# A four-layer conv, scan and attention network, 64 samples on one core: new order of VectorE's four instructions per state pair, ScalarE's table loads and the work around them

## What is computed

```python
# layer 0: 1x1 expand 96 -> 576 + silu, 5x5 depthwise conv with weights mixed per
#          sample + silu, gate (squeeze-excite), 1x1 conv back to 96, residual
# layer 1: group norm, projection to 192, 3x3 depthwise conv + silu -> xc, then
def step(h, inps):                       # 768 channels, n = 16 states each
    u_t, dt, B_t, C_t = inps
    dA = jnp.exp(dt[:, :, None] * A)                         # "decay"
    h = dA * h + (dt * u_t)[:, :, None] * B_t[:, None, :]    # "drive", the scan
    y = jnp.einsum('bdn,bn->bd', h, C_t) + Dv * u_t          # "product", summed over n
    return (h, y)
_, ys = jax.lax.scan(step, h0, xs)       # over the 784 pixels
#          y1 + y2 + y3 + y4, layer norm, times silu(z), projection, residual
# layer 2: layer norm, FFT mixer over the pixels, FFN in fp8/fp16 rounding
# layer 3: layer norm, attention without softmax, FFN
```

## Time and profile before

| | |
|---|---|
| time, median of 3 runs | 22538.34 us (22494.2 to 22542.6) |
| the profiled execution: time; its span | 22505.68 us; 22503.9 us |
| busy share: VectorE, TensorE, ScalarE, GpSimd | 86%, 84%, 69%, 28% |
| granted TensorE clock, mean | 0.894 |
| VectorE per pair | 2 scans of 1.79 and 1.78 us, drive 0.96 us, product 0.96 us |

### The profile page before, as it was taken

How to read it: one execution, slowest core, us unless ns; L and a number is a source line. 1 busy time by engine, 2 the same in 40 slices (tenths; PEclk the granted TensorE clock), 3 DMA queues, 4 the chain that set the end, 5 groups by cost and what they waited for, 6 DMA issues and landing times.

```text
span 22503.9 us, 334261 instructions
## 1 busy us (share of the span) xinstructions
PE 18818.0 (84%) x100834; PEld 6890.1 (31%) x100834; DVE 19251.1 (86%) x17938; ACT 15624.5 (69%) x21098; POOL 6356.1 (28%) x3909
## 2 busy tenths in 40 slices
PE   5888888888888888888888888888888888888887
PEld 1333333333333333333333333333333333333332
DVE  4888888888888888888888888888888888888887
ACT  3767777777677677776776777767767767777674
POOL 1222222222222222222222222222222222222222
PEclk8889898898898998988988889889889898898898
DMA  5555555555555555555555555545555555555552
GB/s 144 143 135 140 140 138 139 135 144 137 132 142 138 137 142 135 143 138 134 140 141 133 140 136 141 140 133 143 138 133 143 139 139 141 134 142 136 134 141 75
DMA packets 1418366, 3083.16 MB, mean 137 GB/s; under 512 B 207812, under 2 KB 786696, under 8 KB 1407859
## 3 DMA queue, kind: packets, MB, share of 16 engines
q1 hardware_dynamic: 1372146, 2992.85, 51.6%
q10 hardware_dynamic: 44032, 64.26, 1.1%
HBM read 2796.25 MB, written 221.51 MB: 134 GB/s over the span
## 4 chain that ended last, share of the span: by engine, by line
issue 67%; POOL 15%; PE 8%; DVE 5%; ACT 4%; DMA 1%; POOLq 0%; ACTq 0%; SPq 0%; DVEq 0%
POOL drive L1576 13%; PE bank L575 3%; DVE state L1381 3%; PE state_sum L575 2%; PE pair L575 2%; POOL taps L1563 2%; ACT work L920 1%; DVE drive L1237 1%; PE scan_sum L575 1%; ACT L920 0%; ACT decay_even L920 0%; DVE work L1237 0%; ACT du L920 0%; DVE prod L1237 0%; ACT decay L920 0%
## 5 line engine op out<-in xcount | busy, mean ns | idle before, releaser
L1576 POOL TENSOR_TENSOR drive<-du,Bb 128x784 f32<-128x784 f32 x3072 | 5689.7, 1852 | 15638.6 <-DVE drive L1237 15638.6
L575 PE MATMUL state_sum<-state,fold 128*64 128x392 f32 x24576 | 5610.5, 585 | 1052.4 <-DVE state L1381 1029.9
L1381 DVE TENSOR_TENSOR_SCAN state<-decay_even,drive 128x784 f32<-128x784 f32 x3072 | 5500.2, 1790 | 128.4 <-ACT decay_even L920 17.6
L1381 DVE TENSOR_TENSOR_SCAN state<-decay,drive 128x784 f32<-128x784 f32 x3072 | 5473.3, 1782 | 0.2 <-POOL drive L1576 0.2
L920 ACT ACTIVATE decay_even<-delta,alog 128x784 f32<-128x784 f32 x3072 | 2821.6, 918 | 3240.8 <-DVE state L1381 3224.0
L1237 DVE TENSOR_TENSOR prod<-state_sum,Cb 128x784 f32<-128x784 f32 x3072 | 2950.6, 960 | 1906.4 <-PE state_sum L575 1902.4
L575 PE MATMUL scan_sum<-prod,fold 128*64 128x392 f32 x12288 | 2990.4, 568 | 1500.0 <-DVE prod L1237 1493.9
L575 PEld LDWEIGHTS state_sum<-state,fold 128*64 128x64 f32 x24576 | 1706.4, 154 | 4427.8 <-issue 2288.4
L575 PE MATMUL bank<-rep,taps 120*32 120x392 f32 x30720 | 2973.9, 514 | 96.1 <-ACT image L920 33.8
L920 ACT ACTIVATE decay<-delta,alog 128x784 f32<-128x784 f32 x3072 | 2890.3, 941 | 115.6 <-issue 72.7
L1237 DVE TENSOR_TENSOR drive<-du,Bb 128x784 f32<-128x784 f32 x3072 | 2943.0, 958 | 18.9 <-DVE work L1237 11.9
(11 more groups left out here) (169 smaller groups left out, 17504.8 us busy)
## 6 DMA issues: line engine op xcount, KB each, us to landing
Bb<-bc_rows SPq DMA_DIRECT2D x3072, 392.0 KB, 4.4
rep<-expanded_images SPq DMA_DIRECT2D x3840, 168.0 KB
Cb<-bc_rows SPq DMA_DIRECT2D x3072, 196.0 KB, 3.6
expanded_images<-image SPq DMA_DIRECT2D x1152, 112.0 KB, 2.5
rep<-conv_in_images SPq DMA_DIRECT2D x1152, 112.0 KB, 3.9
dwo<-in_pww SPq DMA_DIRECT2D x65, 1152.0 KB, 7.3
conv_in_images<-image SPq DMA_DIRECT2D x384, 112.0 KB, 3.2
xc<-xc ACTq DMA_DIRECT2D x384, 98.0 KB, 2.6
```

The source lines that it names most:

```text
L575: return pe.matmul(out, lhsT, rhs, start=start, stop=stop)
L1381: v.tensor_tensor_scan(state[:, j % STATES, :], DP[:, 0:L] if j % 2 == 0 else decay[:, j // 2 % DECAYS, :], drive[:, j % 2, :], 0.0, ALU.m ...
L1576: pool.tensor_tensor(drive[:, j % 2, :], du[:, 2 * s + r, :], Bb[:, b % BSLOTS, :], ALU.mult).then_inc(drive_r.sem, 1)
```

## The change

VectorE's order in pair p becomes scan 2p, drive 2p+2, scan 2p+1, product of pair p-1, with `STATES` = 4; the first even drive of a sample is issued in the last pair of the sample before. GpSimd's odd drive waits for the odd scan before it, since the buffer is no longer free by order alone. TensorE folds pair p first and adds the product of pair p-1 after it. ScalarE makes the odd decay of a pair ahead of its even one and runs one pair ahead. `gates()` loads the Silu table by an instruction of its own, ahead of the wait of the Silu. The group norm's power goes from GpSimd to Ln and Exp on ScalarE; the gate's bias is added by a matmul instead of on VectorE. Nearly all places in the tables and yields of lead and tail are new.

```diff
-STATES = 3
+STATES = 4
...
-CONV_SLOTS = (1, 2, 3, 5, 7, 8, 9, 10, 11, 12, 13, 14, 15, 17, 18, 19, 20, 21, 23, 24, 26)
+CONV_SLOTS = (1, 2, 3, 4, 6, 7, 9, 10, 11, 13, 14, 15, 16, 17, 18, 19, 20, 21, 23, 24, 26)
...
-FAR = {("delta", m, h): slot(k) + SECOND * h for m, k in ((2, 4), (3, 6), (4, 16), (5, 22)) for h in range(2)}
+FAR = {("delta", m, h): slot(k) + SECOND * h for m, k in ((2, 8), (3, 12), (4, 22), (5, 25)) for h in range(2)}
...
-READ_AT = {name: at + 1.8 for name, at in HEAD.items()}
+READ_AT = {name: at + (2.4 if name[0] in ("conv", "conv3", "mix") else 1.8) for name, at in HEAD.items()}
...
 # TensorE
             def scan(i, *between):
                 for p in range(NP):
-                    if p >= 1:
-                        summation(i, p - 1)
-                    elif later(i):
-                        summation(i - 1, NP - 1)
-                    go_on(between, 2 * p + 1)
                     pe.wait_ge(state_r.sem, state_r.at(i, 2 * p + 2))
...
                     last.then_inc(folded.sem, 1)
                     go_on(between, 2 * p + 2)
+                    if p >= 1:
+                        summation(i, p - 1)
+                    elif later(i):
+                        summation(i - 1, NP - 1)
+                    go_on(between, 2 * p + 3)
...
 # ScalarE
+            def gates():
+
+                if table[0] != SILU:
+                    act.preload_act_table_set(SILU)
+                table[0] = SILU
...
             def expanded(i, span, c):
                 yield READ_AT["expand", c]
+                gates()
                 act.wait_ge(bank_filled.sem, bank(span, "expand", c))
...
-                for j in range(0, NU, 2):
-                    decaying(j, DP[:, 0:L], 2, even_r)
-                    go_on(between, j - 1.5)
-                    odd(j + 1)
-                    go_on(between, j - 1)
+            def scan(i, ahead, *between):
+                for j in range(2, NU + 2 if ahead else NU, 2):
+                    for n in (j + 1, j):
+                        if n < NU:
+                            decaying(i, n)
+                        else:
+                            decaying(i + 1, n - NU)
+                        go_on(between, j - 2 if n > j else j - 1)
...
             def gating(i, b):
-                yield 2.95 + 2 * b
+                yield 3.6 + 2 * b
+                gates()
...
 # VectorE
                     if j >= 2 or later(i):
+                        v.wait_ge(drive_r.sem, drive_r.at(i, j))
                         v.wait_ge(state_r.sem, state_r.at(i, j - 1))
...
                 for p in range(NP):
-                    driving(2 * p)
                     scanning(2 * p)
+                    go_on(between, 2 * p)
+                    if p < NP - 1:
+                        driving(i, 2 * p + 2)
+                    elif ahead:
+                        driving(i + 1, 0)
+                    scanning(2 * p + 1)
                     if p >= 1:
                         product(i, p - 1)
                     elif later(i):
                         product(i - 1, NP - 1)
-                    go_on(between, 2 * p)
-                    scanning(2 * p + 1)
                     go_on(between, 2 * p + 1)
...
 # GpSimd
-                yield 64.4
-                pool.wait_ge(g_rs.sem, g_rs.at(i))
-                pool.tensor_tensor(gst[:, 6:7], gst[:, 6:7], eps[0:C, 2:3], ALU.pow).then_inc(g_pw.sem, 1)
...
                 pool.wait_ge(drive_r.sem, drive_r.at(i, j))
+                if j >= 2 or later(i):
+                    pool.wait_ge(state_r.sem, state_r.at(i, j - 1))
```

More of the change, by code:

```diff
@@ L50 @@
 SETUP_LINKS = 51
-LEAD_LINKS = 5
+LEAD_LINKS = 4
 TAIL_LINKS = 2
@@ L98 @@
-FAR = {("delta", m, h): slot(k) + SECOND * h for m, k in ((2, 4), (3, 6), (4, 16), (5, 22)) for h in range(2)}
+HEAD.update({("hidden",): 53.1, ("gate",): 55.1, ("point", 0): 58.1, ("point", 1): 60.3, ("group",): 63.1,
+             ("proj", 0): 67.1, ("proj", 1): 69.1, ("proj", 2): 71.1, ("conv3", 0): 73.1, ("conv3", 1): 75.1, ("conv3", 2): 77.1,
+             ("dbl",): 81.1, ("delta", 0, 0): 84.3, ("delta", 0, 1): 85.1, ("delta", 1, 0): 87.1, ("delta", 1, 1): 89.1,
+             ("mix", 0): 91.1, ("mix", 1): 93.1})
@@ L847, in attention @@
                 yield ATTN_AT
-                pe.wait_ge(o_r.sem, o_r.at(i, 2))
-                yield from norm(i, ATTN_AT, 2, o_r, (2, 2))
+                pe.wait_ge(o_r.sem, o_r.at(i, 1))
+                yield from norm(i, ATTN_AT, 2, o_r, (1, 2))
                 yield ATTN_AT + 4
@@ L983, in head @@
                 yield READ_AT["hidden",]
+                gates()
                 act.wait_ge(bank_filled.sem, bank(span, "hidden"))
-                ac(zse[:, :], P[0:RHID, 0:1], ACT.Silu, bias=seb1[:, :], scale=1.0 / L).then_inc(bank_read.sem, 1)
-                yield 56.5
-                act.wait_ge(bank_read.sem, bank(span, "gate"))
-                ac(sc[:, :], scp[:, :], ACT.Sigmoid).then_inc(sc_r.sem, 1)
+                ac(zse[32:32 + RHID, :], P[32:32 + RHID, 0:1], ACT.Silu, bias=seb1[32:32 + RHID, :], scale=1.0 / L).then_inc(bank_read.sem, 1)
+                yield READ_AT["gate",]
+                act.wait_ge(bank_filled.sem, bank(span, "gate"))
+                ac(sc[:, :], P[:, 0:T0], ACT.Sigmoid).then_inc(bank_read.sem, 1)
                 ac(xin[:, :], xin[:, :], ACT.Identity, bias=bn3[:, 1, :]).then_inc(xb_r.sem, 1)
@@ L1049, in logs @@
             def logs(i, span):
-                yield from log_exp(i, span, 0)
-                yield from log_exp(i, span, 1)
-                yield from log_of(i, 0)
-                yield from log_of(i, 1)
+                for m in range(NEAR):
+                    yield from log_exp(i, span, m)
+                    yield from log_of(i, m)
             def far_logs(i, span):
@@ L1354, in steps, with scan @@
                     tt(du[:, m, :], delta[:, m, :], u_of(m), ALU.mult).then_inc(du_r.sem, 1)
-            def scan(i, *between):
+            def scan(i, ahead, *between):
                 def product(i, p):
@@ L1528, in _ @@
             go_on([Beside(lead(0, (FIRST, 0))), Beside(shares(1))], END)
-            scan(0, Beside(steps(0, NEAR, NK)), Beside(lead(1, (LOOP, 0))), Beside(shares(2)))
+            scan(0, True, Beside(steps(0, NEAR, NK)), Beside(lead(1, (LOOP, 0))), Beside(shares(2)))
             done = SETUP_LINKS + 2 * LEAD_LINKS
```

185 lines of the change are left out of this document (97 added, 88 removed).

## The result

The changed kernel takes 22750.92 us (median; 22735.44 to 22845.87) against 22540.47 us for the kernel before in the same rounds (22494.2 to 22550.52): ratio 1.0112, 95% interval 1.0092 to 1.0131 (the plain quotient of the two medians is 1.0093, inside it). It is 1.1% slower; forecast were 21450 us and 4.7% faster.

What follows compares the result with a forecast made beforehand. VectorE's work and its waits, chiefly the product's for TensorE's fold, were taken to bound the kernel. Terms -1520 - 110 - 410 + 600 + 400 - 20 = -1060 took 22505.7 to 21446, said as 21450 us; range 20600 to 22300.

Steps and rivals of the forecast that it cites:

- The product's room: VectorE's product behind the odd scan gives TensorE's fold 1.7 us more room: -1520 us, bounds -950 and -1902.
- The even scan's wait: Sign of being right: VectorE's even scan waits for ScalarE's `decay_even` some 600 us, up from 17.6.
- Silu loads ahead of waits: ScalarE loading the Silu table before its wait saves at most 34 us, taken as nothing.
- GpSimd's own wait: GpSimd's drive waiting for the odd scan costs nothing, since it ends before the next odd scan begins.
- Places of head and tail: New places put readers about one half-pair behind writers, saving two thirds of 613 us tail waits: -410, bounds -613 and 0.
- GpSimd's drive: Moved behind the odd scan, it delays VectorE's two-SBUF-operand items behind the product: +400 us, bounds 0 and +600.
- norm steps take or wait about 0.9 us more: Sign of being right: VectorE's norm steps behind the product lose about 0.9 us each to GpSimd's reading of SBUF.
- ScalarE's loads: Six added Silu table loads per loop pass make ScalarE late in pairs 3 to 5 and 8 to 11: +600 us, bounds 0 and +1100.
- Hand-over: VectorE's drive waiting for the even scan replaces costlier waits between dependent instructions: -110 us, bounds -200 and 0.
- small gain: Rival: half the product's wait comes back and ScalarE costs its upper bound; 21950 to 22500 us, chance 0.14.
- ScalarE becomes the bound: Rival: four table loads in each of nine pairs hold up even scans, up to 23100 us; slower by over 0.2%, chance 0.12.
- no change: Rival: what VectorE stops waiting for in the product it waits for elsewhere; chance 0.04.

Runs made afterwards that it cites:

- e9: Changed kernel without its own Silu loads, the compiler putting them in as in the kernel before: 22757.51 us, 1.0104 of the kernel before.
- e7: Changed kernel with the places of mixer, ffn and attention as in the kernel before, post's places staying new: 22880.73 us, 1.0161 of the kernel before.
- e13: Changed kernel with the lead's places and the tail's from the mixer on as in the kernel before: 23705.72 us, 1.0541 of the kernel before.
- e1: Changed kernel with VectorE's four waits opening mixer, ffn and attention emitted three half-pairs later, at their norm step: 22697.66 us, 1.0081 of the kernel before.
- e2: Changed kernel with GpSimd's odd drives cut to one column of 784 in all samples but the first: 22493.87 us, 0.9995 of the kernel before.
- e11: Changed kernel with the lead's places (its tables of order, slots, reads and logarithms) as in the kernel before: 23717.56 us, 1.0539 of the kernel before.
- e8: Changed kernel with all of VectorE's items behind the even scan, none behind the product: 22493.51 us, 0.9993 of the kernel before.
- e3: Kernel before with GpSimd's odd drives cut to one column in all samples but the first, as control: 22671.9 us, 1.0065 of the uncut kernel.
- e6: Changed kernel with the gate's three Silus back beside the expands', sharing their loads: 22602.36 us, 1.0038 of the kernel before.
- e12: Changed kernel with the three edits of e10 and the even drive moved behind the odd scan: 21974.62 us, 0.9752 of the kernel before.
- e10: Changed kernel with the edits of e1, e6 and e8 together: 22014.27 us, 0.9772 of the kernel before.

## Why the prediction was wrong

**What held.** The product's room: -1520 forecast, -1603 in the waits. TensorE's wait for `prod` ahead of its adding, 1493.9 us before, is gone (its adding waits 0.5 us); its fold waits for the product in its place, 2514.5 us, as a fold that is early does. The even scan's wait: some 600 forecast, 510.9. About 3700 table loads: 1894 + 1768 and 66 by the compiler, 3728. Silu loads ahead of waits at nothing: shown by e9. GpSimd's own wait at nothing: the odd scan never waits for it (the even scan does, 28.8 us in all). That the table has no drain behind its load: load at 10078.91, Silu at 10080.20.

**The step that failed first: "Places of head and tail", -410.** It took the new places as a gain on the old ones, since a reader stands one half-pair behind its writer. Measured: the tail's waits rose by 473, and a wait that I had not seen at all, without an instruction of its own, cost 283 more at the drive behind it. The rows of VectorE's trace added up by the terms of the prediction show how much hangs on this step. They are -1603 for the product, +473 + 283 where -410 was forecast, +493 for the even scan, and +526 of work: together +172 of the 229.7 us that the span grew (small rows make the rest). The forecast was 1290 us too low, and this term is 1166 of them. e7 shows that the new order brings these waits and the tail's new places don't remove them: all rows named `work` and the drive's wait for `t` together are 769 us in the kernel before, 1548 in the new order with the tail's old places, 1537 with its new ones.

A half-pair is 2.6 us, and the writer's chain is longer: the convolution matmuls that TensorE has ahead of the mean, the mean, Ln and Exp take from 10108.55 to 10113.71 in the timelines above. In the kernel before, the product's long waits stood in these pairs (4.38 us in the earlier trace rows). That they gave that chain its time, and that with them gone the chain shows at the next instruction that needs it, is read from these timelines; no run takes it apart.

**With it falls the sum itself.** It took each wait for time that can be had. e13 shows the contrary: the product's wait fell by 1269 us (the rows of `issue` counted as its own), and VectorE's idle time as a whole rose by 481. e1 freed 283 us of waits for 53 us of time, e2 some 700 us of work for 257. e11 and e7 show what the places are worth in the new order: 4.2% for the lead's, 0.5% for the tail's. They are no term beside the order, but the condition under which it costs only 1.1%.

**GpSimd's drive, +400 (0 to 600).** The mechanism was right, the size too low. What I had counted, instructions with two SBUF operands, came out near: 343 us more in six groups. What I had left out are the FFN's casts, which have one operand, of 16 bits, and take 846 ns instead of 352: 389.5 us. The sign "norm steps take or wait about 0.9 us more" does not single out this cause: they take 0.11 to 0.35 us more on average, and wait for ScalarE 1.26 us more each (L1419 33.9 us, L1446 356.8, 256 steps). In time the lock is worth about 257 us by e2 and e8 alike. Set against its control e3, which became 0.65% slower by the same cut, e2 would give some 400 us; that part stays open.

> The Trainium skill, "SBUF — State Buffer", section "Who interferes with whom", names casts in their two-port modes beside instructions with two SBUF inputs. The prediction used only the second half. The trace agrees with both as to who waits (352 to 846 ns for a cast, 933 to 1994 for the sum with `rbr`); in which mode a cast runs no trace says.

**ScalarE's loads, +600 (0 to 1100).** The place was right (pairs 2 to 4), the size was 150 us by e6 alone. Summed by place in the sample, some 317 of the even scan's 510.9 us of waits lie in pairs 3 to 5, where 5.5 us a sample (346) were forecast; e6 took 295 away. In pairs 8 to 11, where 4 us a sample (252) were forecast, lie 107, all in pair 11; no run tested those by themselves.

**Hand-over, -110.** Wrong in sign as a cost of VectorE: the even scan takes 1.88 us from start to start where it took 1.71, the drive behind it 0.90 instead of 0.98, together 0.10 us more a pair. It is unimportant in time (e12).

**The rivals.** The result lies beyond *small gain* and short of *ScalarE becomes the bound*; the mechanism of the latter is one of three at work. That items wait for each other through three engines, so that a removed wait comes back, I had as *no change* with a chance of 0.04.

Why three edits give more than their sum (by 1.2%, some 270 us) is seen in part: alone, e6 hands 79 us on to the very wait that e1 removes, and e8 hands its gain to the wait of the even scan (913.5 us), which is 622.3 in e10. TensorE's clock may be another part: in e10 it is 0.920, against 0.903 in the changed kernel, and TensorE's same 100962 matmuls take 433 us less, where e1, e6 and e8 by themselves save 101, 40 and 100. No run shows whether the clock shortened the time or the fuller engines raised the clock. What would spread the 37.7 us of TensorE in pairs 24 to 28 stays open too.

## What to carry to other kernels

A wait in the profile is time only if nothing else ends at the same moment: before a wait is summed, look in its own stretch at how full the other engines are, and follow the chain of small items that it covers. When the order of the main loop changes, every reader's distance from its writer changes with it, in microseconds and not in places of the table; find new places (and waits without an instruction) before judging the order: here the same order was 5.4% slower, 1.1% slower or 2.3% faster by places and loads alone. Put items of two SBUF operands, and 16-bit casts, where GpSimd does not read.

## What the runs showed of the hardware

The mean granted TensorE clock differs with the order of work: 0.894 before, 0.903 after, 0.920 in e10, 0.867 in e13, 0.886 in e3. In e3 only GpSimd's work had changed, and TensorE's busy time rose by 157 us for the same 100834 instructions: a control that takes work from one engine can move another engine's clock, and is then no clean control (here it was 0.65% slower). A single-input cast from 16 bits in SBUF waits for GpSimd's drive as two-input instructions do: 846 ns on average against 348 where the drive has one column, with the 378 casts that begin inside a drive ending 218 to 228 ns behind its end.
